# Eight PSUM banks divided anew between two kinds of score tile in a two-layer attention kernel

## The chip, the cores and the metric

The kernel runs on one core of a Trainium2 chip. The time is the device time of one execution in microseconds; the figure of a kernel is the median over several executions. The engines are named as in the profile: PE (TensorE matmuls), PEld (TensorE weight loads), DVE (VectorE), ACT (ScalarE), POOL (GpSimd) and SP, which issues most transfers.

## The reference

The input is 16 sequences of 512 tokens with 128 features. Two layers follow each other. Each adds an attention part and a feed-forward part to the residual:

```
xn = layernorm(x);  x = x + attn0(xn) + ffn0(xn)      # layer 0, causal
xn = layernorm(x);  x = x + attn1(xn) + ffn1(xn)      # layer 1, bias by position

attn0, per head (16 heads of 8): q, k, v through small projections, RMS norm on q and k
    scores = q k^T * scale + causal;  softmax;  @ v
attn1, per head: scores = q k^T * scale + log(exp(-|pos_i - pos_j|) + 1e-8);  softmax;  @ v
ffn0: sigmoid(xr Wr) * (relu(xk Wk)^2 Wv), with xr, xk mixed from each token and the one before
ffn1: gelu(xn W1) W2, where W1 and W2 are composed once from the top 32 primitives
```

## The kernel before, in words

**Batches, units, slots.** Each layer runs 16 batches (sequences). A batch is four units `u` of four heads. A unit is four groups `kt` of four slots, so that a batch has 64 slots. All five engines walk the same slots in programs of their own; each executes its queue strictly in order, and semaphores connect them. A batch's other work (projections, norms, feed-forward, transposes) is spread over the slots by the tables `WORK_USES` and `OTHER_WORK`. Layer 1 begins while the last batches of layer 0 end. Most batches run in a loop, two to a pass.

**Two score matrices.** Softmax wants the maximum of each query's row before the exponential. So PE computes the scores twice. First, two units ahead, with queries as rows: `scores_max` (L587) writes one tile of 128 queries into a bank of `s1`, and DVE reduces it to 128 maxima (L1077 in layer 0, L1082 in layer 1). In layer 0 a causal bias is added by two more small matmuls (L602, L604), and the tile has 128, 256, 384 or 512 columns. The maxima are transposed, copied and written back by DMA as further rows of the stacked queries. Then `scores_t` (L572) computes the scores with keys as rows and the maximum already subtracted into a bank of `st`, ACT takes the exponential into `probs` (L846), POOL masks the diagonal (L1181, layer 0) or multiplies a bias in (L1195, layer 1), and PE multiplies by the values (`pv`, L567) one unit later.

**A slot on PE** is: at the first slot of a group, `pv` of the unit before (8 matmul records); then one `scores_t` tile; then one `scores_max` tile, which lies in the other half of the array's rows and can run beside it; then what the table puts there. Since the queue is in order, a wait at any of these stops all that stand behind it.

**The rings.** PSUM has eight banks of 512 float32. `s1` has four, `st` two, `pv`'s accumulator one and the other work one. PE may write a bank of `st` once ACT has read it (L578: the exponential of the pack two before), and a bank of `s1` once DVE has reduced it (L593: the tile four before). In layer 0, DVE reduces tile by tile. In layer 1 it reduces two banks in one instruction of 1024 columns, with the wait at every second slot (L1079 to L1083).

**Packs.** In layer 0 the tiles of `kt` 1, 2 and 3 have fewer than 512 columns; `PACKS` puts two of them in one bank where they fit (384 + 128, 256 + 256), so that a unit has ten packs, thus ten exponentials, for 16 tiles. In layer 1 each tile is a pack. `place` says in which row of `probs` a pack lands. `TILES` is the order of tiles over the slots, and `BESIDE` derives from it which tile of maxima stands in the same slot (the width is that of the `scores_t` tile beside it).

Of the kernel before, what the change touches and what calls it, by code (L numbers as in the profile page):

```python
# [18 lines left out]
P = 128  # L19
# [3 lines left out]
G = 4  # L23
# [33 lines left out]


PACKS = {
    0: (((0, 0),), ((2, 0), (2, 2)), ((0, 1),), ((1, 0), (3, 0)), ((0, 2),), ((1, 1), (3, 1)), ((0, 3),),  # L60
        ((2, 1), (2, 3)), ((1, 2), (3, 2)), ((1, 3), (3, 3))),
    1: tuple(((kt, j),) for kt in range(NT) for j in (1, 0, 3, 2)),
}
TILES = [[(p, pack, tile) for p, pack in enumerate(PACKS[layer]) for tile in pack] for layer in range(2)]
# [22 lines left out]
def place(layer, kt, j):  # L87

    if layer == 1:
        return G * kt + j, 0, T  # L90
    width = T - P * kt
    row, column = {0: (j, 0), 1: (G + j, 0), 3: (G + j, T - P), 2: (2 * G + j % 2, 2 * P * (j // 2))}[kt]
    return row, column, width
# [169 lines left out]
def build(nc, a, out):  # L263
# [14 lines left out]
    with ExitStack() as ctx:  # L278
# [4 lines left out]
            return ctx.enter_context(nc.semaphore(name))  # L283


        s1 = ctx.enter_context(nc.psum_tensor("scores_for_max", [P, NT, T], F32))
        st = ctx.enter_context(nc.psum_tensor("scores_transposed", [P, 2, T], F32))
        acc = ctx.enter_context(nc.psum_tensor("pv_acc", [P, T], F32))
        work = ctx.enter_context(nc.psum_tensor("work", [P, T], F32))

# [210 lines left out]
        def _(pe):  # L501
# [38 lines left out]
            def body(B):  # L540
# [31 lines left out]
                def scores_t(u, i):  # L572

                    number, pack, (kt, j) = TILES[layer][i]
                    if i == 0:
                        pe.wait_ge(s["mrow_loaded"], B.count(NG * 16 * MROW_DMAS, 16 * MROW_DMAS * (u + 1)))
                    if (kt, j) == pack[0]:
                        wait(pe, s["exp_done"], B.count(NG * EXPS[layer], EXPS[layer] * u + number - 1))  # L578
                    q0 = P * kt if layer == 0 else 0
                    column = place(layer, kt, j)[1]  # L580
                    rows, h, p = slice(HALF * (j % E), HALF * (j % E) + KROWS), (G * u + j) // E, B.parity(0)
                    last = mm(st[:, number % 2, column:column + T - q0], ks[p][rows, h, P * kt:P * kt + P],  # L582
                              qs[p][rows, h, q0:T], start=True, stop=True)
                    if (kt, j) == pack[-1]:
                        last.then_inc(s["st_ready"], 1)

                def scores_max(off, su, i):  # L587

                    if su == 0 and i == 0:
                        pe.wait_ge(s["stack_loaded"], B.count(16 * STACK_DMAS, 16 * STACK_DMAS, off))  # L590
                        if layer == 1 and B.i is None and B.number + off == 0:
                            pe.wait_ge(bias_in, 4 * E * 16)
                    wait(pe, s["red_done"], B.count(64, 16 * su + i - 3, off))  # L593
                    j, qt = BESIDE[layer][i]
                    first = HALF * (j % E)
# [3 lines left out]
                    last = mm(s1[:, i % 4, 0:k1], qs[p][rows, h, P * qt:P * qt + P], ks[p][rows, h, 0:k1],  # L599
                              start=True, stop=(layer == 1))  # L600
                    if layer == 0:
                        mm(s1[:, i % 4, P * qt:k1], ident_halves[half, 0, :], causal_halves[half, 0, :],  # L602
                           start=False, stop=False)
                        last = mm(s1[:, i % 4, P * qt + HALF:k1], ident_halves[half, 1, :],  # L604
                                  causal_halves[half, 1, HALF:P], start=False, stop=True)
                    last.then_inc(s["s1_ready"], 1)

# [130 lines left out]
        def _(act):  # L738
# [8 lines left out]
            def body(B):  # L747
# [87 lines left out]
                for u in range(NG):  # L835
                    for kt in range(NT):
                        for j in range(G):
                            number, pack, tile = TILES[layer][4 * kt + j]
                            if B.has(0) and tile == pack[-1]:
                                if layer == 0 and number == 0:  # L840
                                    wait(act, s["pv_done"], B.count(NG * NT, NT * (u - 1)))
                                if layer == 1 and j == 0:
# [12 lines left out]
                            yield  # L855
# [16 lines left out]
        def _(dve):  # L872
# [67 lines left out]
            def body(B):  # L940
# [126 lines left out]
                for u in range(NG):  # L1067
                    for kt in range(NT):
                        first(u, kt)
                        so, su = (0, u + 2) if u < 2 else (1, u - 2)  # L1070
                        for j in range(NT):
                            m = NT * kt + j
                            if B.has(so) and layer == 0:
                                dve.wait_ge(s["s1_ready"], B.count(64, 16 * su + m + 1, so))
                                jh, qt = BESIDE[0][m]
                                column = max_column(jh, qt)
                                v.reduce_max(maxs[:, su % 2, column:column + 1], s1[:, m % 4, 0:P * (qt + 1)],  # L1077
                                             AX_X).then_inc(s["red_done"], 1)
# [177 lines left out]
```

## Time and profile before

| what | value |
| --- | --- |
| median of 3 runs (lowest to highest) | 2236.93 us (2210.84 to 2249.34) |
| the profiled execution's own time | 2222.09 us |
| its span, mean granted clock of TensorE | 2220.3 us, 0.901 |
| busy share PE / DVE / ACT / POOL | 81% / 73% / 60% / 36% |
| exponentials (L846) | 1664, 947.6 us busy |
| reduces of layer 0 (L1077) / of layer 1 (L1082) | 1024, 447.8 us / 512, 611.1 us |
| first exponentials of layer 0 / 1, by the timeline | at 126 us / 1120 us |

The busy time of PE counts every matmul from its start to its modelled end, so that a lone matmul of 512 columns counts 0.39 us while several in a row follow each other faster. An engine that is busy 73% of the time on average can still be the one waited for in a given slot; the views of waits tell which. Rows are quoted from two steady stretches, 600 to 900 us (layer 0, 200 exponentials at 40 a batch: 5.0 batches) and 1400 to 1700 us (layer 1, 278 exponentials at 64 a batch: 4.34 batches). From them a batch of layer 0 takes 60 us and one of layer 1 69 us.

### The profile page before, as it was taken

How to read it: one execution, taken by the hardware profiler on the slowest of the kernel's cores; microseconds unless marked ns; L12 is line 12 of the kernel's file. 1: busy time of each engine (PE TensorE's matmuls, PEld its weight loads, DVE VectorE, ACT ScalarE, POOL GpSimd, SP SyncE). 2: the span in 40 equal slices, each digit the busy share in tenths (PEclk: the TensorE clock that was granted, in tenths of full speed). 3: DMA queues.
4: the chain of work that ended last, by engine and by line, in shares of the span. 5: the costliest groups of instructions: out<-in, count | busy, mean ns of one | idle time of the engine just before them, and what ended most of it. 6: DMA issues, size and time to landing. Idle time of an engine off the chain costs nothing.

```text
span 2220.3 us, 43213 instructions
## 1 busy us (share of the span) xinstructions
PE 1803.9 (81%) x12618; PEld 737.9 (33%) x12618; DVE 1612.6 (73%) x2911; ACT 1340.5 (60%) x2518; POOL 803.4 (36%) x824
## 2 busy tenths in 40 slices
PE   5888877778787888877588888888888888888885
PEld 2544333334333333332223333233333323323221
DVE  4377776777676676774578888987878878788881
ACT  1256665656555665654267766776767666677763
POOL 2113344433333443333123433442434333343343
PEclk9678999988888898897679999999999999999997
DMA  6222223222122223220322212122122321312200
GB/s 223 41 49 58 59 59 59 59 60 53 41 51 57 35 59 59 59 54 30 59 46 54 52 41 55 34 58 55 42 47 37 54 47 42 54 34 57 50 11 15
DMA packets 136762, 116.97 MB, mean 53 GB/s; under 512 B 20440, under 2 KB 129248, under 8 KB 136544
## 3 DMA queue, kind: packets, MB, share of 16 engines
q1 hardware_dynamic: 129856, 100.65, 22.5%
q0 software_dynamic: 4096, 8.40, 1.2%
q10 hardware_dynamic: 2592, 5.24, 0.7%
q8 instruction: 109, 1.79, 0.4%
q14 instruction: 109, 0.89, 0.2%
HBM read 79.63 MB, written 33.55 MB: 51 GB/s over the span
## 4 chain that ended last, share of the span: by engine, by line
PE 33%; issue 28%; DVE 13%; POOL 11%; DMA 5%; ACT 5%; SPq 4%; DVEq 1%; POOLq 0%; ACTq 0%
PE pv_acc L567 9%; PE scores_transposed L582 8%; POOL probs L1195 7%; DVE maxs L1077 3%; PE work L645 3%; DMA stacks<-mT 3%; ACT probs L846 3%; PE scores_for_max L599 2%; DVE maxs L1082 2%; SPq L433 2%; SPq L451 2%; PE work L695 2%; POOL out_dram L1137 2%; PE work L617 1%; DMA stacks<-parts_scratch 1%
## 5 line engine op out<-in xcount | busy, mean ns | idle before, releaser
L846 ACT ACTIVATE probs<-scores_transposed 128x512 f32<-128x512 f32 x1664 | 947.6, 600 | 501.2 <-PE scores_transposed L582 466.1
L582 PE MATMUL scores_transposed<-stacks 62*128 62x512 bf16 (+3 forms) x2048 | 646.7, 363 | 128.3 <-ACT probs L846 81.8
L599 PE MATMUL scores_for_max<-stacks 60*128 60x512 bf16 (+3 forms) x2048 | 664.8, 366 | 88.1 <-DVE maxs L1082 41.6
L1082 DVE TENSOR_REDUCE maxs<-scores_for_max 128x2 f32<-128x1024 f32 x512 | 611.1, 1219 | 131.2 <-PE scores_for_max L599 126.2
L1077 DVE TENSOR_REDUCE maxs<-scores_for_max 128x1 f32<-128x512 f32 (+3 forms) x1024 | 447.8, 483 | 259.4 <-PE scores_for_max L604 226.6
L1195 POOL TENSOR_TENSOR probs<-probs,near_bias 128x512 f32<-128x512 f32 x256 | 337.3, 1319 | 674.6 <-ACT probs L846 674.1
L567 PE MATMUL pv_acc<-probs,vals 128*32 128x512 f32 (+3 forms) x4096 | 501.7, 565 | 93.0 <-issue 43.1
L582 PEld LDWEIGHTS scores_transposed<-stacks 62*128 62x128 bf16 x2048 | 163.7, 95 | 789.9 <-ACT probs L846 446.5
L1181 POOL TENSOR_SCALAR_AFFINE_SELECT probs<-probs 128x512 f32<-128x512 f32 x256 | 159.3, 641 | 302.1 <-ACT probs L846 301.9
L602 PE MATMUL scores_for_max<-causal_halves,ident_halves 64*128 64x128 bf16 x1024 | 224.7, 233 | 0.0
L599 PEld LDWEIGHTS scores_for_max<-stacks 60*128 60x128 bf16 x2048 | 176.1, 95 | 132.1 <-DVE maxs L1082 66.6
L604 PE MATMUL scores_for_max<-causal_halves,ident_halves 64*128 64x64 bf16 x1024 | 197.5, 199 | 0.0
L567 PEld LDWEIGHTS pv_acc<-probs,vals 128*32 128x32 f32 x4096 | 84.1, 111 | 232.2 <-issue 169.6
L604 PEld LDWEIGHTS scores_for_max<-causal_halves,ident_halves 64*128 64x128 bf16 x1024 | 107.1, 105 | 55.5 <-issue 15.6
L602 PEld LDWEIGHTS scores_for_max<-causal_halves,ident_halves 64*128 64x128 bf16 x1024 | 98.3, 100 | 0.6
L617 PE MATMUL work<-ident,accS 128*128 128x128 f32 x512 | 93.2, 310 | 4.5 <-ACT mT L761 2.4
L1146 POOL TENSOR_TENSOR rstd<-mv,minus_half 128x4 f32<-128x4 f32 x32 | 33.7, 1053 | 163.6 <-DVE mv L988 163.6
L645 PE MATMUL work<-wcat,xnT 128*128 128x512 f32 x128 | 88.6, 780 | 2.3 <-ACT big L782 0.9
L667 PE MATMUL work<-xnT,w 128*128 128x512 f32 x128 | 78.6, 699 | 1.8 <-DVE att L975 0.8
L853 ACT ACTIVATE accS<-pv_acc 128x512 f32<-128x512 f32 x128 | 77.7, 607 | 3.6 <-PE pv_acc L567 3.6
L695 PE MATMUL work<-w,big 128*128 128x128 f32 x512 | 77.5, 297 | 0.0
L972 DVE RECIPROCAL rsum<-work 128x16 f32<-128x16 f32 x128 | 31.9, 249 | 61.9 <-PE work L617 61.8
(126 smaller groups left out, 1901.2 us busy)
## 6 DMA issues: line engine op xcount, KB each, us to landing
stacks<-parts_scratch SPq DMA_DIRECT2D x768, 64.0 KB
parts_scratch<-parts SPq DMA_DIRECT2D x64, 384.0 KB, 3.1
stacks<-mT SPq DMA_DIRECT2D x512, 2.0 KB
x_tile<-in_L_attn_x_dram SPq DMA_DIRECT2D x16, 256.0 KB, 3.8
probs<-in_fc_B_dram ACTq DMA_DIRECT2D x1, 4096.0 KB, 19.8
stage_a<-in_fc_A_T_dram SPq DMA_DIRECT2D x1, 4096.0 KB, 16.5
x_res<-in_L_attn_x_dram SPq DMA_DIRECT2D x16, 256.0 KB, 3.9
x_tile<-x_between_layers SPq DMA_DIRECT2D x16, 256.0 KB, 3.7
```

The lines of the kernel that those rows point to most:

```text
L567: last = mm(acc[32 * j:32 * j + 32, q0:T], vals[:, B.parity(off), kt, G * pu + j, :], probs[:, row, column:column + width], start=(kt == 0 ...
L582: last = mm(st[:, number % 2, column:column + T - q0], ks[p][rows, h, P * kt:P * kt + P], qs[p][rows, h, q0:T], start=True, stop=True)
L599: last = mm(s1[:, i % 4, 0:k1], qs[p][rows, h, P * qt:P * qt + P], ks[p][rows, h, 0:k1], start=True, stop=(layer == 1))
L602: mm(s1[:, i % 4, P * qt:k1], ident_halves[half, 0, :], causal_halves[half, 0, :], start=False, stop=False)
L604: last = mm(s1[:, i % 4, P * qt + HALF:k1], ident_halves[half, 1, :], causal_halves[half, 1, HALF:P], start=False, stop=True)
L645: mm(work[:], xnT[:, B.parity(2), 1 + P * t:1 + P * t + P], wcat[:].rearrange("p a n -> p (a n)"), start=True, stop=True).then_inc(full, 1)
L695: last = mm(work[:, P * t:P * t + P], big[:, f, P * t:P * t + P], w2[:, f, :], start=(f == 0), stop=(f == NF - 1))
L846: fn(probs[:, row, :], st[:, number % 2, :], ACT.Exp, scale=SCALE).then_inc(s["exp_done"], 1)
L1077: v.reduce_max(maxs[:, su % 2, column:column + 1], s1[:, m % 4, 0:P * (qt + 1)], AX_X).then_inc(s["red_done"], 1)
L1082: v.reduce_max(maxs[:, su % 2, :].rearrange("p (e x) -> p e x", e=E)[:, :, column], s1[:, m % 4 - 1:m % 4 + 1, :], AX_X).then_inc(s["red_d ...
L1181: g.affine_select(out=diag, in_=diag, compare_op=ALU.is_ge, fill=0.0, base=0, pattern=[[0, G], [1, P]], channel_multiplier=-1).then_inc(s[ ...
L1195: g.tensor_tensor(diag, diag, near_bias[:, kt, :].unsqueeze(1).broadcast_to([P, G, P]), ALU.mult).then_inc(s["emul_pool"], 1)
```

## The change

`st` gets four banks and `s1` two. ACT takes one exponential of two adjacent banks (1024 columns) for every two packs; PE may write a bank of `st` once the pack four before is done. DVE reduces one bank at a time in both layers, and PE may write a bank of `s1` once the tile two before is reduced. So that two packs of an exponential land in adjacent rows of `probs`, the packs of layer 0 are reordered, and in layer 1 `place` swaps rows pairwise. Exponentials of layer 0 go from ten to five a unit, those of layer 1 from 16 to eight; reduces of layer 1 go from eight to 16.

```diff
 PACKS = {
-    0: (((0, 0),), ((2, 0), (2, 2)), ((0, 1),), ((1, 0), (3, 0)), ((0, 2),), ((1, 1), (3, 1)), ((0, 3),),
-        ((2, 1), (2, 3)), ((1, 2), (3, 2)), ((1, 3), (3, 3))),
+    0: (((0, 0),), ((0, 1),), ((1, 0), (3, 0)), ((1, 1), (3, 1)), ((0, 2),), ((0, 3),),
+        ((1, 2), (3, 2)), ((1, 3), (3, 3)), ((2, 0), (2, 2)), ((2, 1), (2, 3))),
...
-        return G * kt + j, 0, T
+        return G * kt + (j ^ 1), 0, T
...
-        s1 = ctx.enter_context(nc.psum_tensor("scores_for_max", [P, NT, T], F32))
-        st = ctx.enter_context(nc.psum_tensor("scores_transposed", [P, 2, T], F32))
+        s1 = ctx.enter_context(nc.psum_tensor("scores_for_max", [P, 2, T], F32))
+        st = ctx.enter_context(nc.psum_tensor("scores_transposed", [P, 4, T], F32))
...
-                        wait(pe, s["exp_done"], B.count(NG * EXPS[layer], EXPS[layer] * u + number - 1))
+                        wait(pe, s["exp_done"], B.count(NG * EXPS[layer], EXPS[layer] * u + number - 3))
...
-                    wait(pe, s["red_done"], B.count(64, 16 * su + i - 3, off))
+                    wait(pe, s["red_done"], B.count(64, 16 * su + i - 1, off))
...
-                            if B.has(0) and tile == pack[-1]:
+                            if B.has(0) and tile == pack[-1] and number % 2 == 1:
...
-                                row = place(layer, *tile)[0] + (PACK_ROWS * (u % 2) if layer == 0 else 0)
-                                fn(probs[:, row, :], st[:, number % 2, :], ACT.Exp, scale=SCALE
-                                   ).then_inc(s["exp_done"], 1)
+                                row = place(layer, *tile)[0] - 1 + (PACK_ROWS * (u % 2) if layer == 0 else 0)
+                                bank = (EXPS[layer] * u + number) % 4 - 1
+                                fn(probs[:, row:row + 2, :], st[:, bank:bank + 2, :], ACT.Exp, scale=SCALE
+                                   ).then_inc(s["exp_done"], 2)
...
-                            if B.has(so) and layer == 1 and j % 2 == 1:
-                                dve.wait_ge(s["s1_ready"], B.count(64, 16 * su + m + 1, so))
-                                column = max_column(*BESIDE[1][m - 1])
-                                v.reduce_max(maxs[:, su % 2, :].rearrange("p (e x) -> p e x", e=E)[:, :, column],
-                                             s1[:, m % 4 - 1:m % 4 + 1, :], AX_X).then_inc(s["red_done"], 2)
+                                jh, qt = BESIDE[layer][m]
+                                column, width = max_column(jh, qt), P * (qt + 1) if layer == 0 else T
+                                v.reduce_max(maxs[:, su % 2, column:column + 1], s1[:, m % 2, 0:width], AX_X
+                                             ).then_inc(s["red_done"], 1)
```

The order of DVE's instructions in a batch of layer 1, from slot 16 to slot 30, before:

```order
L1058 SCALAR_TENSOR_TENSOR fb<-fa,fd 128x512
L1082 TENSOR_REDUCE maxs<-scores_for_max 128x2
L972 RECIPROCAL rsum<-work 128x16
L975 TENSOR_TENSOR att<-work,rsum 128x4x32
L1064 SCALAR_TENSOR_TENSOR big<-fc,fd 128x512
L1082 TENSOR_REDUCE maxs<-scores_for_max 128x2 x4
```

and in the change:

```order
L1059 SCALAR_TENSOR_TENSOR fb<-fa,fd 128x512
L1078 TENSOR_REDUCE maxs<-scores_for_max 128x1 x2
L973 RECIPROCAL rsum<-work 128x16
L976 TENSOR_TENSOR att<-work,rsum 128x4x32
L1065 SCALAR_TENSOR_TENSOR big<-fc,fd 128x512
L1078 TENSOR_REDUCE maxs<-scores_for_max 128x1 x8
```

The other work stands where it did; each reduce of two tiles has become two, and the wait for the first tile stands one slot earlier.

The order of PE's score matmuls in the first group of a unit of layer 0 (slots 0 to 3; the small L602 and L604 rows stand after each L599), before:

```order
L582 MATMUL scores_transposed<-stacks 128x512
L599 MATMUL scores_for_max<-stacks 128x512
...
L582 MATMUL scores_transposed<-stacks 128x256
L599 MATMUL scores_for_max<-stacks 128x256
...
L582 MATMUL scores_transposed<-stacks 128x256
L599 MATMUL scores_for_max<-stacks 128x256
...
L582 MATMUL scores_transposed<-stacks 128x512
L599 MATMUL scores_for_max<-stacks 128x512
```

and in the change:

```order
L582 MATMUL scores_transposed<-stacks 128x512
L599 MATMUL scores_for_max<-stacks 128x512
...
L582 MATMUL scores_transposed<-stacks 128x512
L599 MATMUL scores_for_max<-stacks 128x512
...
L582 MATMUL scores_transposed<-stacks 128x384
L599 MATMUL scores_for_max<-stacks 128x384
...
L582 MATMUL scores_transposed<-stacks 128x128
L599 MATMUL scores_for_max<-stacks 128x128
```

The widths of a unit's 16 slots were 512, 256, 256, 512 / 384, 128, 512, 384 / 128, 512, 256, 256 / 384, 128, 384, 128 and are 512, 512, 384, 128 / 384, 128, 512, 512 / 384, 128, 384, 128 / 256, 256, 256, 256, for the tiles of the exponentials and of the maxima alike.

## Rows read from the trace of the kernel before

**Rows 1.** Engines in the two steady stretches; columns named in the first line.

```profile
core 0: us, PE busy (x) PEld busy (x) DVE busy (x) ACT busy (x) POOL busy (x), PEclk, DMA share, GB/s
600.00:900.00 300.00, 242.93 (x2170) 112.01 (x2168) 213.22 (x520) 178.60 (x325) 116.60 (x145) 0.89 0.28 55
1400.00:1700.00 300.00, 259.42 (x1502) 92.45 (x1498) 246.87 (x335) 207.38 (x401) 114.18 (x96) 0.95 0.23 47
```

**Rows 2.** Groups of instructions, 600 to 900 us: busy us, mean ns | idle before.

```profile
L846 ACT ACTIVATE probs<-scores_transposed 128x512 f32<-128x512 f32 x200 | 114.2, 594 | 74.0 <-PE scores_transposed L582 63.2 <-remote 8.5 <-issue 1.2
L1077 DVE TENSOR_REDUCE maxs<-scores_for_max 128x1 f32<-128x512 f32 x80 | 54.6, 682 | 39.7 <-PE scores_for_max L604 39.7
L1077 DVE TENSOR_REDUCE maxs<-scores_for_max 128x1 f32<-128x384 f32 x80 | 44.0, 550 | 14.2 <-PE scores_for_max L604 14.0
L1077 DVE TENSOR_REDUCE maxs<-scores_for_max 128x1 f32<-128x256 f32 x80 | 31.1, 416 | 9.6 <-remote 9.4
L1077 DVE TENSOR_REDUCE maxs<-scores_for_max 128x1 f32<-128x128 f32 x80 | 22.6, 283 | 12.2 <-PE scores_for_max L604 11.7 <-issue 0.5
```

**Rows 3.** Groups of instructions, 1400 to 1700 us.

```profile
L1082 DVE TENSOR_REDUCE maxs<-scores_for_max 128x2 f32<-128x1024 f32 x140 | 167.0, 1218 | 31.1 <-PE scores_for_max L599 29.6 <-issue 0.7
L846 ACT ACTIVATE probs<-scores_transposed 128x512 f32<-128x512 f32 x278 | 158.5, 604 | 74.0 <-PE scores_transposed L582 72.9 <-PE pv_acc L567 0.6
```

**Rows 4.** Waits, 600 to 900 us: total us, times, longest us.

```profile
DVE maxs L1077 <- PE scores_for_max L604: 65.4, 66, 2.5
PEld scores_transposed L582 <- ACT probs L846: 45.1, 75, 1.7
PEld scores_for_max L599 <- DVE maxs L1077: 14.5, 13, 1.6
PE scores_for_max L599 <- DVE maxs L1077: 11.7, 13, 1.4
PE scores_transposed L582 <- ACT probs L846: 3.8, 12, 0.4
```

**Rows 5.** Waits, 1400 to 1700 us.

```profile
PEld scores_transposed L582 <- ACT probs L846: 79.6, 118, 1.3
DVE maxs L1082 <- PE scores_for_max L599: 29.6, 18, 4.0
PEld scores_for_max L599 <- DVE maxs L1082: 19.2, 18, 2.2
PE scores_transposed L582 <- ACT probs L846: 15.1, 39, 0.8
PE scores_for_max L599 <- DVE maxs L1082: 12.5, 14, 1.9
```

**Rows 6.** Timeline, PE in a group of layer 1: start, length [idle before].

```profile
1565.85 0.39 PE L582 MATMUL scores_transposed<-stacks 62*128 62x512 bf16 x1
1566.08 0.38 PE L582 MATMUL scores_transposed<-stacks 62*128 62x512 bf16 x1
1566.92 0.39 PE L582 MATMUL scores_transposed<-stacks 62*128 62x512 bf16 x1 [0.47 <-ACT probs L846]
1567.44 0.39 PE L582 MATMUL scores_transposed<-stacks 62*128 62x512 bf16 x1
1567.84 1.06 PE L567 MATMUL pv_acc<-probs,vals 128*32 128x512 f32 x8
```

**Rows 7.** Timeline, ACT in the same group.

```profile
1566.27 1.11 ACT L846 ACTIVATE probs<-scores_transposed 128x512 f32<-128x512 f32 x2 [0.64 <-PE scores_transposed L582]
```

**Rows 8.** Timeline, reduces of 512, 256 and 256 columns in a row, layer 0.

```profile
709.42 1.35 DVE L1077 TENSOR_REDUCE maxs<-scores_for_max 128x1 f32<-128x512 f32 x3 [0.34 <-PE scores_for_max L604]
```

**Rows 9.** Timeline, tiles of 384 and 128 columns and their reduce, layer 0.

```profile
706.02 0.33 PE L599 MATMUL scores_for_max<-stacks 60*128 60x384 bf16 x1
706.28 0.22 PE L599 MATMUL scores_for_max<-stacks 60*128 60x128 bf16 x1
706.48 0.56 DVE L1077 TENSOR_REDUCE maxs<-scores_for_max 128x1 f32<-128x384 f32 x1 [1.03 <-PE scores_for_max L604]
```

More of the change, by code:

```diff
@@ L581, in scores_t @@
                     rows, h, p = slice(HALF * (j % E), HALF * (j % E) + KROWS), (G * u + j) // E, B.parity(0)
-                    last = mm(st[:, number % 2, column:column + T - q0], ks[p][rows, h, P * kt:P * kt + P],
+                    last = mm(st[:, (EXPS[layer] * u + number) % 4, column:column + T - q0], ks[p][rows, h, P * kt:P * kt + P],
                               qs[p][rows, h, q0:T], start=True, stop=True)
@@ L598, in scores_max @@
                     k1 = P * (qt + 1) if layer == 0 else T
-                    last = mm(s1[:, i % 4, 0:k1], qs[p][rows, h, P * qt:P * qt + P], ks[p][rows, h, 0:k1],
+                    last = mm(s1[:, i % 2, 0:k1], qs[p][rows, h, P * qt:P * qt + P], ks[p][rows, h, 0:k1],
                               start=True, stop=(layer == 1))
                     if layer == 0:
-                        mm(s1[:, i % 4, P * qt:k1], ident_halves[half, 0, :], causal_halves[half, 0, :],
+                        mm(s1[:, i % 2, P * qt:k1], ident_halves[half, 0, :], causal_halves[half, 0, :],
                            start=False, stop=False)
-                        last = mm(s1[:, i % 4, P * qt + HALF:k1], ident_halves[half, 1, :],
+                        last = mm(s1[:, i % 2, P * qt + HALF:k1], ident_halves[half, 1, :],
                                   causal_halves[half, 1, HALF:P], start=False, stop=True)
@@ L838, in body @@
                             number, pack, tile = TILES[layer][4 * kt + j]
[L839 to L840 removed]
+                            if B.has(0) and tile == pack[-1] and number % 2 == 1:
+                                if layer == 0 and number == 1:
                                     wait(act, s["pv_done"], B.count(NG * NT, NT * (u - 1)))
[L842 removed]
+                                if layer == 1 and j == 1:
                                     wait(act, s["pv_done"], B.count(NG * NT, NT * (u - 1) + kt + 1))
                                 act.wait_ge(s["st_ready"], B.count(NG * EXPS[layer], EXPS[layer] * u + number + 1))
[L845 to L847 removed]
+                                row = place(layer, *tile)[0] - 1 + (PACK_ROWS * (u % 2) if layer == 0 else 0)
+                                bank = (EXPS[layer] * u + number) % 4 - 1
+                                fn(probs[:, row:row + 2, :], st[:, bank:bank + 2, :], ACT.Exp, scale=SCALE
+                                   ).then_inc(s["exp_done"], 2)
                             eo, eu = (-1, NG - 1) if u == 0 else (0, u - 1)
@@ L1072, in body @@
                             m = NT * kt + j
-                            if B.has(so) and layer == 0:
+                            if B.has(so):
                                 dve.wait_ge(s["s1_ready"], B.count(64, 16 * su + m + 1, so))
[L1075 to L1078, printed above, removed]
-                            if B.has(so) and layer == 1 and j % 2 == 1:
-                                dve.wait_ge(s["s1_ready"], B.count(64, 16 * su + m + 1, so))
-                                column = max_column(*BESIDE[1][m - 1])
-                                v.reduce_max(maxs[:, su % 2, :].rearrange("p (e x) -> p e x", e=E)[:, :, column],
-                                             s1[:, m % 4 - 1:m % 4 + 1, :], AX_X).then_inc(s["red_done"], 2)
+                                jh, qt = BESIDE[layer][m]
+                                column, width = max_column(jh, qt), P * (qt + 1) if layer == 0 else T
+                                v.reduce_max(maxs[:, su % 2, column:column + 1], s1[:, m % 2, 0:width], AX_X
+                                             ).then_inc(s["red_done"], 1)
                             other(16 * u + 4 * kt + j)
```

## The prediction

> **What bounds the kernel now.** I first read the busy time of each engine in one steady stretch of either layer. No engine is full: in layer 1 PE shows 259.4 us of 300, DVE 246.9, ACT 207.4; in layer 0 it is 242.9, 213.2 and 178.6 [rows 1]. So the time is made of hand-overs, and the views to read next are the waits. PE is the engine whose queue holds everything together (scores for ACT, scores for DVE, values, all other matmuls, in order), so its waits count. In layer 0 it waits 45.1 + 3.8 us for ACT to free a bank of transposed scores and 14.5 + 11.7 us for DVE to free a bank of maxima [rows 4]. With 5.0 batches in that stretch this is 9.8 and 5.2 us a batch. In layer 1 it is 79.6 + 15.1 us for ACT and 19.2 + 12.5 us for DVE [rows 5], with 4.34 batches 21.8 and 7.3 us a batch. ACT's ring of two banks is the tight one now, and the change loosens just that. But DVE is the busier of the two consumers: in layer 1 only 18 of 140 reduces waited for PE [rows 3, 5], the others found their tiles ready; and the change gives DVE the tight ring.
>
> The timeline shows what the tight ring does to a group of four slots in layer 1 [rows 6, 7]. PE starts the first tile at 0 (1565.85) and the second 0.23 later. The first exponential starts at 0.42 and the third tile must wait for its end: 1.07. The fourth comes at 1.59, the values' matmuls at 1.99. Without the ring the fourth would start at 0.69, so a clean group holds 0.90 us of waiting, 16 groups 14.4 of the 21.8 us a batch. The other 7.4 us come from ACT being at something else.
>
> **The change part by part, layer 1.** *PE's wait for ACT* goes: a tile now waits for the pair of packs before the last pair. That pair's exponential starts 0.42 after its second tile and takes about 1.11, what two in a row take now [rows 7]; nothing shows one of 1024 columns, and it lies between one single (0.604, [rows 3]) and two of them. A group with its values' matmuls (1.06, [rows 6]) lasts longer than that, so in a clean group this wait is nil.
>
> *DVE's ring takes its place.* A single reduce of 512 columns takes 0.682 [rows 2], and consecutive ones overlap by 0.09 (three of 0.68, 0.42 and 0.42 took 1.35, [rows 8]), so they follow each other every 0.60. How long after the start of a tile a single reduce starts in layer 1 is in no row; ACT's 0.42 [rows 7] and layer 0's 0.46, with its added bias matmuls [rows 9], are the nearest, and I take 0.42. Then, 0.05 us for the release included each time, as between an exponential and the tile it frees, the first reduce runs 0.42 to 1.10, the third tile starts near 1.15, the second reduce runs 1.02 to 1.70, and the fourth tile starts at 1.75 against 1.59 now. A clean group waits 1.06 instead of 0.90, 17.0 us a batch instead of 14.4.
>
> *Other work behind the tight ring.* Apart from the ring's own instructions a batch of layer 1 has (207.4 - 158.5) / 4.34 = 11.3 us on ACT and (246.9 - 167.0) / 4.34 = 18.4 us on DVE [rows 1, 3]. Behind a ring of two tiles ACT's 11.3 caused those 7.4 us of waiting; in proportion DVE's 18.4 cause 12.0. The ring of two pairs, with DVE's other work behind it, costs 7.3 us now; with ACT's it should cost 7.3 x 11.3 / 18.4 = 4.5. What queues behind a waiting maximum tile on PE is all of it: the next transposed scores, the other matmuls and the values, thus ACT and POOL too.
>
> Layer 1 then has 17.0 + 12.0 + 4.5 = 33.5 us of PE waits a batch against 29.1 now: +4.4.
>
> *Splitting the reduce* by itself: two singles cost 2 x 0.682 - 1.218 = 0.15 us more than a double when they stand alone [rows 2, 3], but 2 x 0.60 - (1.218 - 0.09) = 0.07 back to back. For 512 pairs that is 36 to 75 us of DVE time; the walk holds it as the pitch of 0.60. The Trainium skill (VectorE: DVE Perf Modes, section on the TRN2 errata) gives a PSUM-sourced DVE instruction 120 cycles beside one per column, so splitting costs 125 ns a pair whatever the neighbours do; that speaks against the change harder than my row. By that rule the pitch would be 0.66 and the sum some 8 us higher. Rows 8, where a part of the fixed cost overlaps, go before it.
>
> **Layer 0.** The four-bank ring of single reduces becomes a two-bank one. From the start of a tile to its reduce it is 0.46, and slots can follow each other at 0.26 [rows 9]. Walking the four groups with 0.68, 0.55, 0.42 and 0.28 for the four widths [rows 2], 0.60 for an exponential and the packs' old and new order, the fourth tile starts at:
>
> ```
> group widths now           before  after
> 512, 512, 384, 128          1.07    1.78
> 384, 128, 512, 512          1.33    1.32
> 384, 128, 384, 128          1.33    1.32
> 256, 256, 256, 256          0.78    1.26
> ```
>
> In the first group the old order had a pack of 256 + 256 in the middle, so the third pack came only at the fourth slot, while DVE's ring does not know packs: it counts tiles, 16 a unit against ten. Against 0.78 without waits a unit waits 2.56 instead of 1.39 us, a batch 10.2 instead of 5.6. ACT's 9.8 measured less 5.6 leaves 4.2 for its other work (12.9 us a batch; DVE's is 12.2, [rows 1, 2]). After: DVE keeps the 5.2 that it causes even with four banks (the long chunks: mixing, norm, means) and adds 4.2 x 12.2 / 12.9 = 4.0 for the lost two; ACT keeps between 0 and 4.2, I take 1.0 as its packs reach over six slots. 10.2 + 9.2 + 1.0 = 20.4 against 15.0: +5.4 a batch.
>
> *At nothing:* POOL's masks (the exponentials of `kt` 0, 1 and 3 come earlier, those of `kt` 2 at the last slot, still eight slots ahead of their values), the rows in `probs`, the DMA of the maxima (a unit ahead). If the last exponential came half a unit late, the third `pv` would wait. The fill and the border of the layers hold about two batches without one ring or the other; I count 16 batches for each.
>
> **The sum.** A wait is not all lost time: a weight load can be idle beneath a matmul still running. PE's matmuls are idle 40.6 us of 300 in layer 1 [rows 1], 9.4 a batch against 29.1 of waits, a third; the other bound is the whole. I take half. (4.4 + 5.4) x 16 / 2 = 78 us, on the profiled execution's own 2222: **2300 us**. A third gives 2274, the whole 2379. The profiled execution lies 15 us under the median of the runs shown, and the forecast is 2.8% over that median. About 2% (45 us) is what a measurement can tell from no change.
>
> **The rivals.** *Faster: ACT is released and DVE keeps up.* This needs DVE's other work to fall into PE's absences (`pv`, other matmuls), so that its waits do not grow from 5.2 in layer 0 and 7.3 in layer 1, ACT's other-work waits vanish, and the single reduce, free of the wait for a second tile, frees the fourth tile as early as ACT does now. Layer 0: 10.2 + 5.2 - 15.0 = +0.4; layer 1: 14.4 + 7.3 - 29.1 = -7.4; by halves -56 us, **2166 us**. For it: the waits for ACT are three times those for DVE, and DVE waits for PE 65.4 us in layer 0 [rows 4], so it has room there. Against: the 122 of 140 reduces that found their tiles waiting. It decides if DVE's own waits in layer 1 stay under 10 us a batch. Chance 0.23.
>
> *An even trade.* One ring's waits replace the other's, other terms cancel: 2220 to 2260, say **2235**. For it: the clean groups of layer 1 differ by only 0.16 us. Chance 0.25.
>
> *Far slower.* PE's gaps become whole losses (2379), or the clock falls with them: the granted clock is 0.95 of full in layer 1 and 0.89 in layer 0, whose groups are more broken up [rows 1], a mean over stretches at 2.4 and at 1.2 GHz. If layer 1 went to 0.89, its 55 us a batch outside waits would grow by 6.7%, 3.7 us, 59 in all: **2359**. The Trainium skill (TensorE: Matmul & The Clock Gate, section on psum-queue depth-cycling) describes such a kernel, in which cycling through banks leaves small gaps and the clock swings. Chance 0.10.
>
> The forecast itself has 0.42.
>
> **How the numbers follow.** 2300 is the likeliest case, whose own range is 2265 to 2345, seven parts of 42 below 2282. So slower by over 2%: 0.35 + 0.10 = 0.45. Within 2%: 0.07 + 0.24 = 0.31. Faster: 0.23 + 0.01 = 0.24. The range 2180 to 2375 leaves out most of the faster case and the far end of the far slower one, 0.18 in all.
>
> **What would show it.** In the waits of the changed kernel, PE's for ACT before the transposed scores should fall from 94.7 us in 300 to under 25 in layer 1, and those for DVE rise from 31.7 to over 100; in layer 0 DVE's from 26 to over 80. In the timeline of a clean group of layer 1 the third and fourth tile should start near 1.15 and 1.75 after the first, released by DVE. A single reduce in layer 1 should mean 0.68 us, an exponential about 1.1, ACT's busy time fall below DVE's share by more than now. The forecast is wrong if DVE shows most of its reduces waiting for PE, or if PE's waits for DVE do not reach twice today's.

## The result

The changed kernel takes 2454.6 us (median of four, 2444.9 to 2463.1) against 2223.9 of the kernel before beside it: 1.114 times as long, 95% interval 1.103 to 1.126. The forecast was 2300, range 2180 to 2375. The direction was right, the size three times too small, and even the range's end was passed by 80 us.

### The profile page after: what moved, and what is told of

Same layout as the page of the kernel before. It is cut to its first block, busy times and chain, and to the rows that moved or that the text cites. A ratio compares the mean times of both kernels' runs of the same rounds, so it can differ in the third digit from the quotient of the medians.

```text
span 2461.3 us, 42916 instructions
## 1 busy us (share of the span) xinstructions
PE 2013.9 (82%) x12618; PEld 764.3 (31%) x12618; DVE 1640.9 (67%) x3423; ACT 1268.3 (52%) x1686; POOL 801.9 (33%) x824
## 3 DMA queue, kind: packets, MB, share of 16 engines
q1 hardware_dynamic: 129856, 100.65, 20.4%
## 4 chain that ended last, share of the span: by engine, by line
PE 46%; issue 20%; DVE 19%; POOL 5%; ACT 4%; DMA 3%; SPq 2%; DVEq 1%; POOLq 0%; ACTq 0%
PE pv_acc L567 12%; DVE maxs L1078 10%; PE scores_transposed L582 9%; PE scores_for_max L599 7%; POOL probs L1191 3%; PE work L667 2%; PE work L645 2%; PE work L695 2%; PE work L635 2%; ACT probs L847 2%; DMA stacks<-mT 2%; PE scores_for_max L602 1%; PE work L661 1%; SPq L451 1%; DMA stacks<-parts_scratch 1%
## 5 line engine op out<-in xcount | busy, mean ns | idle before, releaser
L1078 DVE TENSOR_REDUCE maxs<-scores_for_max 128x1 f32<-128x512 f32 (+3 forms) x2048 | 1127.5, 585 | 633.9 <-PE scores_for_max L604 368.3
L847 ACT ACTIVATE probs<-scores_transposed 128x1024 f32<-128x1024 f32 x832 | 846.1, 1024 | 594.8 <-PE scores_transposed L582 591.4
L599 PE MATMUL scores_for_max<-stacks 60*128 60x512 bf16 (+3 forms) x2048 | 727.5, 383 | 282.0 <-DVE maxs L1078 266.5
L582 PE MATMUL scores_transposed<-stacks 62*128 62x512 bf16 (+3 forms) x2048 | 662.9, 375 | 10.5 <-DMA stacks<-mT 6.7
L567 PE MATMUL pv_acc<-probs,vals 128*32 128x512 f32 (+3 forms) x4096 | 537.2, 602 | 67.7 <-POOL probs L1177 29.2
L599 PEld LDWEIGHTS scores_for_max<-stacks 60*128 60x128 bf16 x2048 | 175.9, 96 | 552.3 <-DVE maxs L1078 526.0
L602 PE MATMUL scores_for_max<-causal_halves,ident_halves 64*128 64x128 bf16 x1024 | 244.1, 246 | 0.0
L604 PE MATMUL scores_for_max<-causal_halves,ident_halves 64*128 64x64 bf16 x1024 | 209.7, 208 | 0.0
L604 PEld LDWEIGHTS scores_for_max<-causal_halves,ident_halves 64*128 64x128 bf16 x1024 | 114.2, 112 | 57.3 <-issue 23.0
L602 PEld LDWEIGHTS scores_for_max<-causal_halves,ident_halves 64*128 64x128 bf16 x1024 | 103.3, 103 | 7.9 <-issue 4.9
L761 ACT ACTIVATE mT<-work 32x128 bf16<-32x128 bf16 x128 | 32.9, 257 | 106.0 <-PE work L622 106.0
L782 ACT ACTIVATE big<-work 128x512 f32<-128x512 f32 x64 | 38.2, 597 | 86.2 <-PE work L645 86.2
L829 ACT ACTIVATE parts<-work 128x512 bf16<-128x512 f32 x64 | 38.3, 599 | 82.4 <-PE work L661 64.2
L854 ACT ACTIVATE accS<-pv_acc 128x512 f32<-128x512 f32 x128 | 76.8, 600 | 6.6 <-PE pv_acc L567 6.5
```

What stands on the lines that cost most here:

```text
L567: last = mm(acc[32 * j:32 * j + 32, q0:T], vals[:, B.parity(off), kt, G * pu + j, :], probs[:, row, column:column + width], start=(kt == 0 ...
L582: last = mm(st[:, (EXPS[layer] * u + number) % 4, column:column + T - q0], ks[p][rows, h, P * kt:P * kt + P], qs[p][rows, h, q0:T], start= ...
L599: last = mm(s1[:, i % 2, 0:k1], qs[p][rows, h, P * qt:P * qt + P], ks[p][rows, h, 0:k1], start=True, stop=(layer == 1))
L602: mm(s1[:, i % 2, P * qt:k1], ident_halves[half, 0, :], causal_halves[half, 0, :], start=False, stop=False)
L604: last = mm(s1[:, i % 2, P * qt + HALF:k1], ident_halves[half, 1, :], causal_halves[half, 1, HALF:P], start=False, stop=True)
L847: fn(probs[:, row:row + 2, :], st[:, bank:bank + 2, :], ACT.Exp, scale=SCALE).then_inc(s["exp_done"], 2)
```

## The profile after

The profiled execution took 2463.1 us at a granted clock of 0.860 (before 0.901). The page's first part and the groups that answer to [rows 2, 3]:

```profile
span 2461.3 us, 42916 instructions
PE 2013.9 (82%) x12618; PEld 764.3 (31%) x12618; DVE 1640.9 (67%) x3423; ACT 1268.3 (52%) x1686; POOL 801.9 (33%) x824
...
L1078 DVE TENSOR_REDUCE maxs<-scores_for_max 128x1 f32<-128x512 f32 (+3 forms) x2048 | 1127.5, 585 | 633.9 <-PE scores_for_max L604 368.3
L847 ACT ACTIVATE probs<-scores_transposed 128x1024 f32<-128x1024 f32 x832 | 846.1, 1024 | 594.8 <-PE scores_transposed L582 591.4
L599 PE MATMUL scores_for_max<-stacks 60*128 60x512 bf16 (+3 forms) x2048 | 727.5, 383 | 282.0 <-DVE maxs L1078 266.5
```

DVE's reduces gained only 69 us of busy time (447.8 + 611.1 before), ACT's exponentials lost 101. Both consumers are less busy by share than before. Work is not where the time went; PE's waits for DVE grew. From here on I compare ten batches of each layer, from the first maximum tile of batch 4 to that of batch 14. They took 603.4 and 692.8 us before (60.3 and 69.3 a batch) and 675.9 and 791.8 now (67.6 and 79.2). The waits in layer 1, before and then after, and in layer 0 after:

```profile
PEld scores_transposed L582 <- ACT probs L846: 185.0, 276, 1.3
PEld scores_for_max L599 <- DVE maxs L1082: 40.5, 39, 2.3
PE scores_transposed L582 <- ACT probs L846: 35.7, 91, 1.0
PE scores_for_max L599 <- DVE maxs L1082: 26.4, 30, 1.9
```

```profile
PEld scores_for_max L599 <- DVE maxs L1078: 221.7, 273, 2.6
DVE maxs L1078 <- PE scores_for_max L599: 167.6, 160, 3.8
PE scores_for_max L599 <- DVE maxs L1078: 104.0, 157, 2.1
PEld scores_transposed L582 <- ACT probs L847: 53.9, 65, 1.7
```

```profile
PEld scores_for_max L599 <- DVE maxs L1078: 102.5, 154, 2.7
PE scores_for_max L599 <- DVE maxs L1078: 64.2, 99, 2.5
PEld scores_transposed L582 <- ACT probs L847: 29.3, 24, 1.7
```

The swap took place as forecast: in layer 1 PE waits 32.6 us a batch for DVE instead of 6.7 and 5.4 for ACT instead of 22.1. (These figures add the waits of PE and PEld, as the prediction did.) A clean group of layer 1 shows the ring (start, length; compare [rows 6]):

```profile
2153.82 0.39 PE L582 MATMUL scores_transposed<-stacks 62*128 62x512 bf16 x1
2153.83 0.39 PE L599 MATMUL scores_for_max<-stacks 60*128 60x512 bf16 x1
...
2155.03 0.39 PE L599 MATMUL scores_for_max<-stacks 60*128 60x512 bf16 x1
2155.26 0.38 PE L582 MATMUL scores_transposed<-stacks 62*128 62x512 bf16 x1
2155.63 0.39 PE L599 MATMUL scores_for_max<-stacks 60*128 60x512 bf16 x1
2155.95 1.06 PE L567 MATMUL pv_acc<-probs,vals 128*32 128x512 f32 x8
```

The third tile of maxima starts 1.20 after the first, the fourth 1.80 (I had 1.15 and 1.75). But such groups are rare: of the 160 groups of the ten batches only 2 have their fourth tile of maxima within 1.9 us of the first, against 34 before, and the median rose from 2.29 to 3.04. In a group like it some 550 us earlier, the first matmuls ran at the lower level of the clock:

```profile
1605.97 0.60 PE L582 MATMUL scores_transposed<-stacks 62*128 62x512 bf16 x1
...
1607.39 0.43 PE L599 MATMUL scores_for_max<-stacks 60*128 60x512 bf16 x1
1607.66 0.38 PE L582 MATMUL scores_transposed<-stacks 62*128 62x512 bf16 x1
1607.99 0.39 PE L599 MATMUL scores_for_max<-stacks 60*128 60x512 bf16 x1
...
1606.64 2.51 DVE L1078 TENSOR_REDUCE maxs<-scores_for_max 128x1 f32<-128x512 f32 x4 [1.23 <-PE scores_for_max L599]
```

The first tile takes 0.60 instead of 0.39, so DVE starts later, and third and fourth tile of maxima come at 1.42 and 2.02. And in an ordinary group DVE's other work lies in the ring, here two reduces among three other instructions, and PE behind them:

```profile
1600.97 0.73 DVE L962 TENSOR_SCALAR msp<-maxs 128x16 bf16<-128x16 f32 x1
1601.74 0.18 DVE L964 SCALAR_TENSOR_TENSOR msp<-maxs,msp 128x16 bf16<-128x16 f32 x1
1601.83 0.69 DVE L1078 TENSOR_REDUCE maxs<-scores_for_max 128x1 f32<-128x512 f32 x1
1602.44 0.68 DVE L1053 TENSOR_TENSOR parts<-rest,parts 128x512 bf16<-128x512 f32 x1
1603.04 0.68 DVE L1078 TENSOR_REDUCE maxs<-scores_for_max 128x1 f32<-128x512 f32 x1
```

```profile
1602.58 0.39 PE L599 MATMUL scores_for_max<-stacks 60*128 60x512 bf16 x1 [0.30 <-DVE maxs L1078]
1602.81 0.38 PE L582 MATMUL scores_transposed<-stacks 62*128 62x512 bf16 x1
1603.78 0.39 PE L599 MATMUL scores_for_max<-stacks 60*128 60x512 bf16 x1 [0.60 <-DVE maxs L1078]
```

Each tile that PE writes starts 0.06 us after a reduce ends (1602.52 to 1602.58, 1603.72 to 1603.78), and each reduce stands behind other work.

## The experiments

Ratios are to the kernel before on the same chip, with 95% intervals. Clock and batch times are those of the one profiled execution: the clock of the whole and of the ten-batch stretch of each layer, the batch times of these stretches. Not all kernels ran on the same chip, so that they are best compared by their ratios.

| kernel | ratio | clock | layer 0, 1: clock | layer 0, 1: us a batch |
| --- | --- | --- | --- | --- |
| before | 1 | 0.90 | 0.89, 0.96 | 60.3, 69.3 |
| the change | 1.114 (1.103 to 1.126) | 0.860 | 0.81, 0.91 | 67.6, 79.2 |
| two banks for DVE alone | 1.119 (1.108 to 1.129) | 0.855 | 0.81, 0.92 | 67.8, 76.8 |
| reduce split, four banks | 1.017 (1.006 to 1.027) | 0.915 | 0.90, 0.97 | 60.4, 69.6 |
| three and three | 1.023 (1.012 to 1.034) | 0.890 | 0.89, 0.93 | 59.7, 71.6 |
| three and two | 1.024 (1.016 to 1.032) | 0.890 | 0.88, 0.94 | 60.6, 72.9 |
| change, single exponentials | 1.120 (1.111 to 1.129) | 0.843 | 0.77, 0.92 | 70.1, 77.2 |
| change, wait ahead of both tiles | 1.126 (1.119 to 1.133) | 0.843 | 0.80, 0.89 | 69.2, 80.9 |
| change, half maximum tiles and reduces in layer 1 | 1.048 (1.042 to 1.055) | 0.865 | 0.81, 0.95 | 67.3, 69.5 |
| before, half reduces in layer 1 | 0.987 (0.981 to 0.993) | 0.913 | 0.90, 0.98 | 60.4, 65.9 |
| before, half exponentials in layer 1 | 0.980 (0.973 to 0.987) | 0.898 | 0.87, 0.97 | 60.9, 65.7 |
| two banks, filler in 2 slots of 4 | 1.108 (1.097 to 1.118) | 0.885 | 0.84, 0.97 | 68.1, 75.5 |
| two banks, filler in 1 slot of 4 | 1.148 (1.136 to 1.160) | 0.844 | 0.79, 0.92 | 72.3, 78.6 |
| third part on POOL | 0.990 (0.984 to 0.995) | 0.915 | 0.91, 0.98 | 59.8, 66.9 |
| the same, rings by layer | 0.998 (0.995 to 1.002) | 0.914 | 0.89, 0.98 | 60.4, 67.3 |

### DVE's ring of two banks alone

```diff
-                    wait(pe, s["red_done"], B.count(64, 16 * su + i - 3, off))
+                    wait(pe, s["red_done"], B.count(64, 16 * su + i - 1, off))
...
-                    last = mm(s1[:, i % 4, 0:k1], ...
+                    last = mm(s1[:, i % 2, 0:k1], ...
```

and the single reduces of the change. All else is as before.

> The kernel before with one part of the change: the ring of the scores for the maximum has two banks and single reduces in both layers; two banks and single exponentials for the transposed scores stay, two banks lie idle. Theory A (the depth of DVE's ring is the cause, every microsecond that PE waits for it is lost, and the clock falls with the gaps): as slow as the whole change or slower, since ACT's ring is tight too: 2440 to 2530 us, waits of PE for DVE of 30 us a batch in layer 1, granted clock 0.85 to 0.87. Theory B (the pairs of exponentials hold POOL and the values back, or the new order of packs costs): under 2290 us.

2470.7 us: the whole loss, with the old order of packs, single exponentials and two banks for ACT. The layer 1 waits:

```profile
PEld scores_transposed L582 <- ACT probs L846: 180.4, 280, 1.4
DVE maxs L1077 <- PE scores_for_max L599: 158.9, 162, 3.7
PEld scores_for_max L599 <- DVE maxs L1077: 111.7, 145, 2.3
PE scores_for_max L599 <- DVE maxs L1077: 67.1, 89, 2.0
PE scores_transposed L582 <- ACT probs L846: 40.5, 105, 1.0
```

Here PE waits 22.1 us a batch for ACT and 17.9 for DVE. DVE's wait is below the 30 expected; the run with single exponentials below, in which ACT's ring is wide, has 33.2, so here ACT's wait, which stands before it in the same slot, hides a part of it.

### Splitting the reduce, four banks

Only the single reduces, `s1[:, m % 4, ...]`; PE's wait as before.

> The kernel before with only the double reduce of layer 1 split into two singles; four banks stay. Theory A: 2200 to 2245 us, no change that counts, since two reduces in a row cost 0.07 us more than a double and give banks back sooner. Theory C (the splitting itself costs, by 0.15 us a pair on the path, and a wait more): 512 pairs, +75 us, 2290 to 2310.

2244.4 us, at the upper edge of theory A and well under theory C: a ratio of 1.017, a small cost (24 us by the medians). In the ten-batch stretch of layer 1 it is 0.3 us a batch. So the depth of the ring, not the number of reduces, is the cause of the loss. The waits moved all the same, from 22.1 to 31.1 us a batch for ACT and from 6.7 to 1.2 for DVE, of which ACT's part is in these rows:

```profile
PEld scores_transposed L582 <- ACT probs L846: 241.7, 330, 2.4
PE scores_transposed L582 <- ACT probs L846: 69.0, 140, 1.5
```

The sum rose by 3.5 us a batch and the batch by 0.3: here too a microsecond of waiting is not one of time.

### Three banks each, and three and two

```diff
+                    wait(pe, s["red_done"], B.count(64, 16 * su + (i - 2 if i > 2 else (0, -2, -1)[i]), off))
```

with bank `i % 3`; for three banks of transposed scores the same with `exp_done` and `number % 3`.

> Three banks for either kind of scores, all taken one by one (single exponentials, single reduces, old order of packs). Theory A: between: PE waits less for ACT than before and less for DVE than in the change; 2180 to 2290 us, clock 0.88 to 0.91. If a ring's cost fell off only from four banks on, it would lie above 2350.

> Three banks for the maxima, two for the transposed scores (one bank idle), all taken one by one: beside the kernel with three and three it gives the worth of one more bank for ACT alone. Theory D (PE's waits for ACT are worth little, since DVE's wait or other work stands where they stood): 2255 to 2290 us, within 1% of three and three. The forecast's rule (half a microsecond for each of waiting) gives some 12 us of wait a batch more and so +90 us, about 2350.

2262.3 and 2285.4 us. DVE's banks, all with single reduces and two for ACT, give per batch of layer 0 60.4, 60.6 and 67.8 us with four, three and two, and of layer 1 69.6, 72.9 and 76.8. Layer 0 has a cliff between three and two, layer 1 loses with each. The granted clock went down in step: 0.90, 0.88, 0.81 and 0.97, 0.94, 0.92. The third bank for ACT took its waits in layer 1 from 28.2 to 13.1 us a batch, DVE's rose from 7.2 to 14.7, and a batch gained 1.35. The forecast's rule gave this bank 90 us. The medians differ by 23, but on two chips, and the ratios (1.023 and 1.024) not at all: what it is worth can't be told from nothing.

### The change with single exponentials

The condition `number % 2 == 1` goes, ACT takes bank `(EXPS[layer] * u + number) % 4` alone and counts one.

> The change with single exponentials over the four banks (each pack freed and handed on by itself), all else as in the change. Theory A: 2430 to 2470 us, as the change, waits of PE for DVE unchanged. Theory B in its first form (pairs hold POOL and the values back): under 2350 us.

2479.4 us, 9 above the expectation. By the whole time the pairs hold nobody back (1.114 with them, 1.120 without; in the two stretches a batch of layer 0 is 2.5 us longer without them, one of layer 1 2.0 us shorter). Beside the run with DVE's ring alone it gives the worth of ACT's third and fourth bank, together with the new order of packs, while DVE has two: none (1.120 against 1.119). The waits in layer 1 say where the relief went:

```profile
PEld scores_for_max L599 <- DVE maxs L1077: 222.3, 266, 2.6
PE scores_for_max L599 <- DVE maxs L1077: 109.6, 171, 2.1
PEld scores_transposed L582 <- ACT probs L846: 80.2, 101, 1.4
```

ACT's went from 22.1 to 8.0 us a batch, DVE's from 17.9 to 33.2: the sum from 40.0 to 41.2. PE no longer stops at the first wait of a slot and stops at the second. Layer 0 is not so clean: there the sum fell from 26.6 to 22.0 us a batch, and yet the batch took 70.1 us instead of 67.8, at a clock of 0.77 instead of 0.81.

### The wait ahead of both tiles of a slot

```diff
+                            if B.has(so):
+                                wait(pe, s["red_done"], B.count(64, 16 * su + 4 * kt + j - 1, so))
                             if B.has(0):
                                 scores_t(u, 4 * kt + j)
```

> The change with PE's wait for DVE's bank moved from between the two score tiles of a slot to ahead of both, where the wait for ACT stood. Theory E (the wait is dear because it splits tiles that could run side by side in the array, and the wait for ACT is cheap because it does not): 2380 to 2425. If the place of the wait in the slot does not matter: 2440 to 2490, as ACT now gets its tile later too.

2512.1 us, slower than either form expected; beside the change (1.126 against 1.114) the intervals overlap. I had thought that DVE's wait is dear because it parts two tiles that can run side by side. It is not so: with the tiles kept together nothing was gained. This theory fell.

### Shorter reduces, shorter exponentials

`T // 2` columns for the reduces of layer 1 in the change, and for PE's tiles of maxima too (`k1`); `0:T // 2` in the double reduces of the kernel before, whose tiles keep their 512 columns; 256 columns in its exponentials. These kernels leave out half of the keys, or of the probabilities.

> The change, but the reduces of layer 1 read 256 of a tile's 512 columns (0.42 instead of 0.68 us; the maxima are then not those of all keys). Theory A (DVE's service time behind two banks is what layer 1 waits for): a batch of layer 1 falls from 79 to 70 us or less, PE's waits for DVE from 33 to under 15 us a batch, and the whole to 2280 to 2340. If pairs of exponentials or the latency from PE to DVE were the cause: above 2400.

> The kernel before, but the double reduces of layer 1 read 2 x 256 columns (0.68 instead of 1.22 us, 17 us of DVE time a batch; the maxima are not those of all keys). In the change the same cut gave 9.7 us a batch. Theory A (four banks hide DVE's service time, two do not): a batch falls by 0 to 3 us, 2175 to 2225. If DVE's service time bounds layer 1 whatever the ring: -8 us or more a batch, under 2100.

> The kernel before, but the exponentials of layer 1 cover 256 of 512 columns (some 0.24 us less each, 15 us of ACT time a batch; half of the probabilities are then stale). Theory D (PE's waits for ACT were nearly free: other work of PE, the array still running or DVE stood right behind them): a batch of layer 1 falls by at most 2 us, 2185 to 2225 in all. By the forecast's rule (half a microsecond back for each of the 22 us of waiting, most of which would go): -7 us or more a batch, 2110 or less.

2334.7, 2198.1 and 2182.1 us. In the change DVE's busy time in layer 1 fell by 15.7 us a batch and the batch by 9.7: 0.62 for each. With four banks it fell by 13.9 and the batch by 3.4: 0.24. Two banks thus seem to lay DVE's service time on the path, while four hide most of it, if not all. But the pair is not clean. In the change PE's tiles were halved as well (a matmul took 0.30 us instead of 0.43 on average), and the clock of the stretch rose from 0.91 to 0.95, with four banks only from 0.96 to 0.98:

```profile
1495.14:2286.93 791.79, 668.58 (x3446) 208.38 (x3442) 594.12 (x1081) 447.64 (x601) 261.45 (x220) 0.91 0.21 41
1466.68:2161.94 695.26, 581.88 (x3442) 203.92 (x3441) 437.52 (x1077) 443.26 (x600) 255.59 (x220) 0.95 0.22 47
```

So 0.62 is an upper bound for DVE's service time alone. PE's waits for DVE in the changed kernel only fell to 23.9 us a batch, not under 15; a likely reason, which no run here isolates, is that the way from PE to DVE and back is no shorter. ACT's 12.8 us less in the kernel before gave 3.6 (0.28): more than theory D allowed, half of what the forecast's rule gave. Each consumer has a moderate worth there: while DVE keeps four banks, shorter exponentials do pay.

### A filler matmul

```diff
+                    if i % 4 >= 2:
+                        part = slice(HALF * (j % E), HALF * (j % E) + HALF)
+                        mm(s1[:, i % 4, :].rearrange("p (a b n) -> p a b n", a=2, b=2), ident_halves[part, 0, :],
+                           ident_halves[part].unsqueeze(1).broadcast_to([HALF, 2, 2, P]),
+                           start=True, stop=True)
                     wait(pe, s["red_done"], B.count(64, 16 * su + i - 1, off))
```

The second run has `i % 4 == 3`.

> The kernel with a two-bank ring of maxima alone (2471 us), and in two of four slots one more matmul of 512 columns into a bank that nobody reads, ahead of the wait for DVE: it fills PE's waits. Clock theory (the fall of the granted clock from 0.90 to 0.855 is a part of the loss): the clock rises to 0.87 or more and the time does not rise, 2420 to 2470. Without it: 32 such matmuls a batch at 0.21 us, +0 to +105 us, 2471 to 2576, clock as it was.

> The kernel with the two-bank ring of maxima alone, with the filler matmul only in the last slot of each group, ahead of the wait for DVE: 16 a batch. Clock theory: the clock rises by 0.01 to 0.02 and each 0.01 is worth some 17 us, as between executions of one kernel, while the fillers lie in waits: 2420 to 2460. Without it 2465 to 2500.

2465.4 and 2554.4 us. The first did what the clock theory said, the second missed it by 94 us: with 16 fillers a batch the clock fell to 0.844, with 32 it rose to 0.885, as the ten-batch stretches of layer 0 show, with 32 and then with 16:

```profile
357.15:1038.44 681.29, 585.03 (x4665) 263.86 (x4662) 432.94 (x1040) 362.24 (x650) 233.21 (x291) 0.84 0.23 48
```

```profile
374.36:1097.79 723.43, 602.58 (x4505) 265.06 (x4502) 428.81 (x1040) 361.31 (x650) 233.96 (x291) 0.79 0.23 45
```

I cannot say why one filler lowers the clock. A filler in every slot has no measured time. The kernel with 160 more matmuls in the stretch is 42 us faster in it, at a clock 0.05 higher; over the whole kernel it is 89 us for 0.041. That is no price of the clock, however: beside the kernel without fillers the one with 16 is 84 us slower at a clock only 0.011 lower, so that these fillers cost time by themselves.

More telling is layer 1 of the kernel with 32, here behind that of the kernel before and of the one with two banks and no filler:

```profile
1349.60:2042.38 692.78, 594.24 (x3442) 212.50 (x3441) 567.19 (x762) 477.58 (x920) 263.44 (x221) 0.96 0.24 47
1518.96:2286.95 767.99, 654.87 (x3441) 215.22 (x3441) 582.20 (x1079) 478.25 (x920) 263.59 (x220) 0.92 0.22 42
1512.09:2266.69 754.60, 647.94 (x3762) 218.76 (x3761) 584.98 (x1081) 478.44 (x920) 264.56 (x220) 0.97 0.22 44
```

With two banks the clock is back at 0.97, and a batch still takes 75.5 us against 69.3: 6.2 of the 7.5 us that the ring cost remain. How much of these the fillers themselves take was not measured.

### The third part on POOL, and rings by layer

In layer 1 `third_part` moves from DVE's program to POOL's. The second kernel also takes three and three banks in layer 0, from one array of six.

> The kernel before with the third part of the split of q and k in layer 1 computed by POOL, as in layer 0, instead of DVE (two instructions of 0.68 to 1.8 us a batch). DVE has some 3 us a batch less, POOL is at 38%: between no change and -2 us a batch, 2190 to 2225.

> As e11, and the rings by layer: three banks for each kind in layer 0 (a batch took 59.7 against 60.3 us), four and two with the double reduce in layer 1. Another -0.6 us x 16 batches: 2180 to 2215, some 10 us under e11.

2215.5 and 2223.0 us. The first has a ratio of 0.990, clear of 1 by its interval but within 2% of no change; the medians of all executions (2215.5 and 2227.4) differ by 0.5% only. It is a small gain at most. DVE's busy time in layer 1 falls by 2.3 us a batch. The rings by layer bring nothing more (0.998; 8 us above the expected range); layer 0's 59.7 us with three and three was no gain that repeats.

## Why the prediction was wrong

**Right.** What bounds the kernel (hand-overs around PE's queue), that DVE's ring takes ACT's place, and the walk of a clean group (1.20 and 1.80 for 1.15 and 1.75). The waits too: forecast after the change 20.4 us a batch in layer 0 and 33.5 in layer 1, measured 19.6 and 38.0. Of the signs named beforehand one fell short: in 600 to 900 us of layer 0 PE waited 75.6 us for DVE, not over 80. The pitch of single reduces held, 0.60 forecast from [rows 8] and not the 0.66 beside it: four in a row took 2.51 us, 0.61 from start to start with the last one whole (0.68). The exponential of 1024 columns takes 1.024 us, not the 1.1 of two in a row, but close to it.

**The step that failed** is the sum: one price, half, for every microsecond of waiting, so that the removed waits for ACT paid for most of the new ones for DVE. By that step DVE's new waits (5.2 to 19.4 and 7.3 to 29.0 us a batch) cost 35.9 x 16 / 2 = 287 us, and ACT's lost ones (9.8 to 1.0 and 21.8 to 4.5) gave back 26.1 x 16 / 2 = 209. Measured, DVE's ring alone costs 250 us: near what was charged, though by luck, since its waits for DVE grew by 24.5 us a batch and not by 35.9. ACT's two more banks, the pairs and the new order together give back 16 us by the medians (2470.7 to 2454.6), with intervals that overlap; without the pairs they give none. The credit was not there. Two waits in one in-order queue are not a sum: the first hides part of the second, and when the first is taken away the second grows. Layer 1 of the change with single exponentials shows it one to one (their sum was 40.0 and then 41.2 us a batch); layer 0, whose clock fell as well, does not.

A whole microsecond for each of waiting would not have been the right price either. On the measured waits of both layers (14.2 us a batch more) it gives 227 us for the change, which took 231; but for two banks for DVE alone (23.2 more) it gives 371 against 250, and for the split reduce (4.3 more) 69 against 24. That it fits the change is chance.

The rows could have warned: of the 140 double reduces in 300 us only 18 waited for PE [rows 5], so behind most waits for ACT there stood a DVE that was late already. I used this for the direction and not for the size.

**The clock** was given a chance of 0.10 as a case of its own. It came together with the likeliest case, whose sum put it at nothing: 0.901 to 0.860 in the profiled executions. Between 30 executions of the unchanged kernel on one chip, from 2204.9 us at 0.913 to 2248.3 at 0.892, a line through them gives 16 us for each 0.01. For 0.041 that is an estimate of some 65 of the 231 us. A bound follows from the spans: at 0.901 the 2220.3 us before are 220 us short of the full clock, at 0.860 the 2461.3 after are 345 short. So even if the matmuls' speed decided every moment, the clock would explain no more than some 125 of the 241 us between the two profiled executions (an estimate); the rest is waiting. By the same working it is at most 4.4 of the 9.9 us a batch in layer 1, where the kernel with 32 fillers points the same way, but 6.2 of the 7.3 in layer 0. In layer 0 the two are not separated: no kernel here lowers the clock without changing the waits. The rule of the Trainium skill that I cited (TensorE: Matmul & The Clock Gate, psum-queue depth-cycling) describes such a case, and the traces agree as far as they go: every profiled kernel with a ring of two banks for DVE lies at 0.843 to 0.865 (0.885 with two fillers a group), every one with three or four at 0.890 to 0.915.

**Smaller steps.** Splitting the reduce was put at 36 to 75 us of DVE time; alone it makes the kernel 1.7% slower (0.6 to 2.7%), 38 us by that ratio and 24 by the medians. The new order of packs in layer 0, to which my walk gave 0.7 us of a unit's first group, was not isolated: with the old order and the same ring for DVE a batch takes 67.8 us, with the new 67.6 with pairs and 70.1 without.

**Open** is why the clock fell, what lowers it with one filler, and how the loss of layer 0 divides between clock and waits; and whether ACT's ring would be worth more while DVE keeps four banks, which needs nine banks and was not tried.

## What to carry to other kernels

In this kernel one in-order engine feeds two consumers through rings of buffers. The spare buffers were worth more with the busier one, and shortening one wait gave back nothing where the next in the queue belonged to an engine that was already late. Read the consumer's own idle time before its instructions: the one that hardly ever waits for the feeder is the one not to squeeze. Price each wait apart, if need be by a kernel that tightens one ring alone, and ask what more gaps do to TensorE's granted clock.

## What the runs showed of the hardware

One activation over two adjacent PSUM banks of 512 columns takes 1.024 us and two in a row took 1.11 [rows 7]; merging them all took 101 us off ACT's busy time and, while DVE had two banks, none off the kernel's within what was measured. Between executions of this kernel 0.01 of TensorE's mean granted clock goes with 16 us. Matmuls whose results nobody reads, put ahead of a wait, can raise it at no loss of time (32 a batch: 0.855 to 0.885, ratio 1.119 to 1.108) or go with a lower clock and a loss (16 a batch: 0.844, ratio 1.148).
